# Second cross attention with halved Fourier products, and the last experts' routing done inside the last cross attention

## The reference, cut to what matters

```python
# layer 1, cross attention, on the normalised x (queries) and ctx_1024 (keys, values)
Q = (queries @ wq).reshape(Bv, Lv, H, Dh).transpose(0, 2, 3, 1)
K = (keys @ wk).reshape(Bv, Lv, H, Dh).transpose(0, 2, 3, 1)
corr = jnp.fft.irfft(jnp.fft.rfft(Q, axis=-1) * jnp.conj(jnp.fft.rfft(K, axis=-1)), n=Lv, axis=-1)
top_vals, top_idx = jax.lax.top_k(corr, k_top)          # k_top = 5
# softmax of the five, then five rolled copies of V, mixed by these weights, @ wo

# layer 3, cross attention: linear attention, 16 heads of 16
q = jax.nn.elu(q) + 1.0
k = jax.nn.elu(k) + 1.0
S = jnp.einsum('bhle,bhld->bhed', k, q)
out = jnp.einsum('bhme,bhed->bhmd', v, S)
denom = jnp.einsum('bhld,bhld->bhl', q, k) + 1e-06
return out @ Wo + bo

# layer 3, experts, on the normalised result: one of 8 experts for each token
logits = flat @ Wr
top_vals, top_idx = jax.lax.top_k(logits, TOP_K)
weights = jax.nn.softmax(top_vals, axis=-1)
top1, w_top1 = top_idx[:, 0], weights[:, 0]
h = gelu(flat @ W1[top1]); y_sel = h @ W2[top1]
out = (w_top1[:, None] * y_sel)
```

## Time and profile before

| | us |
|---|---|
| median of 3 runs | 3126.3 (3125.74 to 3130.65) |
| the profiled execution, its own time | 3151.78 |
| its span | 3149.9 |
| second cross attention, first load to the next stage | 1255.4 to 1512.9 |
| last cross attention | 2573.9 to 2763.1 |
| last experts, routing part up to the first expert product | 2763.96 to 2855.9 |
| last experts, tiles | 2855.9 to 3149.9 |

### The profile page before, as it was taken

How to read it: one execution, slowest core, us unless ns; L and a number is a source line. 1 busy time by engine, 2 the same in 40 slices (tenths; PEclk the granted TensorE clock), 3 DMA queues, 4 the chain that set the end, 5 groups by cost and what they waited for, 6 DMA issues and landing times. The chain is left out here.

```text
span 3149.9 us, 58131 instructions
## 1 busy us (share of the span) xinstructions
PE 2890.9 (92%) x20825; PEld 2309.4 (73%) x20826; DVE 1708.3 (54%) x4515; ACT 1203.7 (38%) x2278; POOL 508.5 (16%) x820
## 2 busy tenths in 40 slices
PE   7979999999997999899789789999799989977998
PEld 6866666666665888788678656666588877777998
DVE  4546777777775011577666477777322237752111
ACT  1325555555553121454334435445333223322221
POOL 1111121111110000000455401110000011041111
PEclk9989999999998999999789889999899999958999
DMA  3049900000000443100214410000111100035553
GB/s 119 0 172 393 367 2 0 0 0 0 0 0 1 171 148 119 30 17 17 85 63 145 128 40 27 20 20 1 63 54 53 54 19 1 0 145 182 178 176 122
DMA packets 126689, 246.54 MB, mean 78 GB/s; under 512 B 17132, under 2 KB 76908, under 8 KB 120176
## 3 DMA queue, kind: packets, MB, share of 16 engines
q1 hardware_dynamic: 116688, 219.72, 20.2%
q0 software_dynamic: 9888, 25.38, 2.2%
HBM read 149.14 MB, written 97.75 MB: 78 GB/s over the span
## 5 line engine op out<-in xcount | busy, mean ns | idle before, releaser
L507 DVE TENSOR_REDUCE m0hnm<-banks 128x4 f32<-128x1024 f32 x256 | 312.9, 1222 | 173.8 <-PE banks L435 173.7
L534 ACT ACTIVATE m0hpT<-banks 128x1024 f32<-128x1024 f32 x256 | 263.1, 1028 | 356.1 <-PE banks L448 356.1
L435 PE MATMUL banks<-m0hk,m0hq 32*128 32x256 f32 x2048 | 293.3, 404 | 12.1 <-DVE m0hnm L507 11.7
L448 PE MATMUL banks<-m0hq,m0hk 32*128 32x256 f32 x2048 | 292.3, 402 | 1.1 <-ACT m0hpT L534 1.1
L532 ACT ACTIVATE a2hpT<-banks,a2hlow 128x512 f32<-128x512 f32 x256 | 162.2, 684 | 191.1 <-PE banks L448 191.1
L435 PEld LDWEIGHTS banks<-m0hk,m0hq 32*128 32x128 f32 x2048 | 176.5, 186 | 64.5 <-DVE m0hnm L507 33.4
L507 DVE TENSOR_REDUCE a2hnm<-banks 128x4 f32<-128x1024 f32 x128 | 156.6, 1223 | 87.5 <-PE banks L435 87.5
L448 PEld LDWEIGHTS banks<-m0hq,m0hk 32*128 32x128 f32 x2048 | 178.2, 185 | 2.1 <-issue 1.7
L435 PE MATMUL banks<-a2hk,a2hq 32*128 32x256 f32 x1024 | 147.8, 406 | 24.7 <-DVE a2hnm L507 24.6
L3083 PEld LDWEIGHTS banks<-E3xT,E3w 128*128 128x128 f32 x1248 | 147.8, 195 | 2.0
L3083 PE MATMUL banks<-E3xT,E3w 128*128 128x128 f32 x1248 | 147.9, 278 | 0.0
(11 more groups left out here) (479 smaller groups left out, 6430.8 us busy)
## 6 DMA issues: line engine op xcount, KB each, us to landing
E3w<-in_L_ffn_W_dram SPq DMA_DIRECT2D x47, 1024.0 KB, 4.9
slots<-M0pad SPq DMA_DIRECT2D x8, 4290.0 KB, 34.4
slots_x<-M0pad SPq DMA_DIRECT2D x8, 4290.0 KB, 36.4
E0w<-in_L_ffn_fw_dram SPq DMA_DIRECT2D x64, 512.0 KB
E2w<-in_L_ffn_w_dram SPq DMA_DIRECT2D x16, 1024.0 KB
E1xin<-slots SPq DMA_DIRECT2D x71, 130.0 KB
A2routed<-routed SPq DMA_DIRECT2D x16, 512.0 KB
E3xin<-slots_x SPq DMA_DIRECT2D x39, 130.0 KB
```

The source lines that it names most:

```text
L435: ins = pe.matmul(self.scores[:, j, tc], self.q[strip(half, j), u, e, c, chunk(tc)], self.k[strip(half, j), u, e, c], start=True, stop=True)
L448: ins = pe.matmul(self.turned[:, j, kc], self.k[strip(half, j), u2, e2, c2, chunk(kc)], self.q[strip(half, j), u2, e2, c2], start=True, st ...
L507: v.tensor_reduce(self.nm[:, e, :, at:at + 33:32].rearrange("p c g -> p g c"), self.scores, AX.X, ALU.max, negate=True).then_inc(self.nm_r ...
L534: ins = a.activation(dst, self.turned, ACT.Exp)
```

## The change

**In the second cross attention** the Fourier products are split. GpSimd forms the sum and the difference of the two token halves of `xn` (into `xs`) and of the context (into `cs`). The even frequencies need only the sum and the odd ones only the difference, so each of the two products takes 128 rows in place of 256 (`halved`). The correlation goes to two PSUM banks and is copied in two halves. Statistics and normalisation of batch b+2 stand earlier in VectorE's turn. At the start each engine waits only for the loads that it needs.

**In the last layer** attention and routing are one function, `layer3`. Slot b of the attention also takes batch b-1 or b-2 through statistics, normalisation (now on ScalarE), transposes, router products, and at fixed slots through `route`, `ranks` and `place` for the groups of batches 0 to 3, 4 to 7 and 8 to 11; the rows of batches 0 to 9 are scattered in slots 7, 8, 11, 12 and 15. Batches 12 to 15 are routed in two groups of two behind a barrier, where the rows of batches 10 to 15 are scattered. All slots are written out, with no loop. GpSimd computes the reciprocal deviation before it waits for the value product. The output bias is added to `x` on GpSimd (`bias`), not on VectorE. Half of the second expert weights are loaded during the attention, into memory that the earlier layers have left.

```diff
 # layer1_attention
+            def halves(dst, src):
+                g.tensor_tensor(dst[:, 0], src[:, 0], src[:, 1], ALU.add)
+                return g.tensor_tensor(dst[:, 1], src[:, 0], src[:, 1], ALU.subtract)
+            def fold_x(b):
+                g.wait_ge(xn_rdy, b + 1)
+                if not (isinstance(b, int) and b == 0):
+                    g.wait_ge(fx_mm, b)
+                halves(xs, xn).then_inc(xs_rdy, 1)
+            def fold_c(b):
+                g.wait_ge(c_in, 16 * b + 16)
...
+                halves(cs, ctx_in).then_inc(cs_rdy, 1)
...
             def body(b, one, two):
                 if two:
                     norm(b + 2)
+                    fold_x(b + 2)
+                    fold_c(b + 2)
...
-            v.wait_ge(w_in, 16 * loads)
-            ch.start(0)
-            stats(0)
...
+                if two:
+                    stats(b + 2)
                 v.wait_ge(ex_rdy, b + 1)
...
                 ins.then_inc(blk_rdy, 1)
                 if two:
-                    stats(b + 2)
+                    apply(b + 2)
                 v.wait_ge(blkT_mm, b + 1)
...
                 if one:
                     first(b + 1)
-                if two:
-                    apply(b + 2)
...
+            def halved(j, src):
+                for m in range(C):
+                    for e in range(2):
+                        last = pe.matmul(bank(j)[:, m].rearrange("p (r e j) -> p r e j", r=2, e=2)[:, :, e], src[:, e, chunk(m)],
+                                         dft_f[:, e].rearrange("p (r j) -> p r j", r=2), start=True, stop=True)
+                return last
...
-                product(pe, lambda m: bank(0)[:, m], lambda k, m: xn[:, k, chunk(m)],
-                        lambda k: dft_f[:, k]).then_inc(fx_mm, 1)
+                halved(0, xs).then_inc(fx_mm, 1)
+                pe.wait_ge(cs_rdy, b + 1)
+                halved(1, cs).then_inc(fc_mm, 1)
 # layer3: constants
+    GROUPS = ((0, 4), (4, 8), (8, 12), (12, 14), (14, 16))
+    routed_at = {hi + 1: g for g, (lo, hi) in enumerate(GROUPS) if hi + 2 < B}
+    placed_at = {slot + 1: g for slot, g in routed_at.items()}
+    rows_at = {7: (0, 1), 8: (2, 3), 11: (4, 5), 12: (6, 7), 15: (8, 9)}
 # layer3, attention, GpSimd
+                def bias(b):
+                    g.wait_ge(fr.xn_rdy, b + 1)
+                    g.tensor_tensor(env.x[:, b], env.x[:, b], tg_bo[:].unsqueeze(1).broadcast_to([P, C, D]), ALU.add).then_inc(bias_rdy, 1)
+                for b in range(-1, B):
+                    if b + 1 < B:
+                        bias(b + 1)
+                    if b + 3 < B:
+                        fr.rstd_of(g, b + 3, (b + 3) % 2)
+                    if b >= 1:
+                        root(g, b - 1)
+                    for r in rows_at.get(b, ()):
+                        scatter(g, r)
+                    if b + 3 < B:
+                        g.wait_ge(v_mm, b + 2)
+                        fr.context(g, b + 3, (b + 3) % 2)
 # VectorE, in slot b
-                for c in range(C):
-                    last = v.tensor_tensor(y[:, u, c], T3[u][:, c], bo[:], ALU.add)
...
+                    if b >= 1:
+                        v.wait_ge(y_used, b + 2)
+                        stats(v, b - 1)
...
+                    if b in routed_at:
+                        route(v, ch, routed_at[b])
+                    if b in placed_at:
+                        place(v, ch, placed_at[b], ranked(b))
 # ScalarE, in slot b
+                    if b >= 2:
+                        rows_turned(a, b - 2, T0[nu])
...
+                    if b >= 2:
+                        take_logits(a, b - 2, T0[nu])
...
+                    if b >= 1:
+                        normalise(a, b - 1)
+                    for r in rows_at.get(b, ()):
+                        rows_of(a, r)
 # TensorE, in slot b
+                    if b >= 2:
+                        turn(pe, b - 2, T0[nu])
...
+                        logits(pe, b - 2, T0[nu])
...
+                    if b in placed_at:
+                        pe.wait_ge(lg_rdy, b - 1)
+                        ranks(pe, placed_at[b], ranked(b))
 # layer3, behind the barrier, TensorE
+                turn(pe, 14, bank(0))
+                logits(pe, 14, bank(0))
+                ranks(pe, 3, ranked(3))
+                turn(pe, 15, bank(1))
+                logits(pe, 15, bank(1))
+                ranks(pe, 4, ranked(4))
```

More of the change, by code:

```diff
@@ L1419, in take @@
                     a.wait_ge(o_mm, b)
[L1420 to L1424, removed]
+                copy(vw_mm, b + 1, vw[:], 5, vw_rdy)
+                for c in range(C):
+                    a.wait_ge(co_mm, 2 * b + c + 1)
+                    a.activation(corr[:, c, 0:S], co_bank(c), ACT.Copy).then_inc(co_rdy, 1)
             take(0)
@@ L1464, in correlate @@
                 pe.wait_ge(sp0_rdy, b + 1)
-                product(pe, lambda m: bank(4)[:, m], lambda k, m: sp_[:, k, chunk(m)],
-                        lambda k: dft_g[:, k]).then_inc(co_mm, 1)
-            pe.wait_ge(w_in, 16 * loads)
+                for m in range(C):
+                    for k in range(C):
+                        last = pe.matmul(co_bank(m), sp_[:, k, chunk(m)], dft_g[:, k], start=(k == 0), stop=(k == C - 1))
+                    last.then_inc(co_mm, 1)
             front(0)
@@ L2719, in layer3_experts @@
         side, token = sb("side", [P, N, 4]), sb("token", [P, N])
[L2720 removed]
+        lg = sb("lg", [P, N, E])
+        hot, eq, pos = (sb(n, [P, GN, E]) for n in ("hot", "eq", "pos"))
         m1, m2, wt, posf = (sb(n, [P, GN]) for n in ("m1", "m2", "wt", "posf"))
[L2722 to L2725 removed]
@@ new lines, in normalise, with rows_turned @@
+        def normalise(a, b):
+            a.wait_ge(rstd_rdy, b + 1)
+            if b >= 2:
+                a.wait_ge(xl_mm, b - 1)
+            for c in range(C):
+                last = a.activation(xf[:, b % 2, c], env.x[:, b, c], ACT.Identity, scale=rstd[:, b % 2, c:c + 1],
+                                    bias=shift[:, b % 2, c:c + 1])
+            last.then_inc(xf_rdy, 1)
+        def rows_turned(a, b, turned):
+            a.wait_ge(xl_mm, b + 1)
+            if b >= 2:
+                a.wait_ge(lg_mm, b - 1)
+            a.activation(xl[:, b % 2], turned, ACT.Copy).then_inc(xl_rdy, 1)
@@ new lines, in turn, with logits @@
+        def turn(pe, b, turned):
+            pe.wait_ge(xf_rdy, b + 1)
+            if b >= 2:
+                pe.wait_ge(xl_rdy, b - 1)
+                pe.wait_ge(lg_rdy, b - 1)
+            transpose4(pe, turned, xf[:, b % 2], env.ident[:]).then_inc(xl_mm, 1)
+        def logits(pe, b, turned):
+            pe.wait_ge(xl_rdy, b + 1)
+            for tc in range(C):
+                for k in range(C):
+                    last = pe.matmul(turned[:, 0, tc * E:tc * E + E], xl[:, b % 2, k, chunk(tc)], wr[:, k],
+                                     start=(k == 0), stop=(k == C - 1))
+            last.then_inc(lg_mm, 1)
```

1099 lines of the change are left out of this document (555 added, 544 removed).

## The result

The changed kernel takes 3078.55 us (median of 4 runs, 3077.34 to 3081.97) against 3126.02 (4 runs, 3122.35 to 3130.65): the ratio is 0.9851, 95% interval 0.9835 to 0.9867, so 47.5 us less. The forecast was 3070, 56 less.

The account below looks back on a forecast made before the run. It took TensorE's work to bound the second cross attention, and a 92 us chain without expert products the routing. Start -9, turns -9, last attention +20, routing -57.6 sum to -56: 3126.3 becomes 3070, range 3048 to 3103.

Parts of the forecast that it names:

- Start, -9: Second cross attention's start: statistics no longer wait for loads, so the stage starts 9 us earlier, between -6 and -10.
- Turn, -0.6 each, -9: Second cross attention: shorter Fourier products, less GpSimd's delay of VectorE, make a turn 13.8 us; -9 over 15 turns.
- the pair's 0.25: Second cross attention's turn: each of GpSimd's four sums delays VectorE 0.25 us, as a profiled pair beside a copy; +1.0.
- The upper bound: Second cross attention's turn: VectorE stands still through all four sums, +2.9 less slack 0.3, turn 15.7, +20 us.
- that rival: Second cross attention: shared port held whole, turn 15.7, 3090 in all; or turn 16.2 and 3100; chance 0.14.
- 13.1 without contention: Second cross attention: GpSimd's sums cost VectorE nothing, turn 13.1, stage -29, 3059 in all; chance 0.25.
- Slot, +0.75: Last cross attention: added transposes and router products partly fill the wait for `sm`; +0.75 us a slot, 14 slots, +10.
- Ranks, route, last scatters, +4 +1 +4 and bias +1: Last cross attention: ranks +4 us, `route` in three slots +1, slot 15's four scatters +4, GpSimd's bias +1.
- The ring: Last cross attention: slots become as long as a ring of waits across engines; total above 3120 us; chance 0.04.
- Tail, 34.6: Routing behind the barrier: first expert product after 34.6 us against 92.2, -57.6; SyncE and first rows' landing 14.4.
- the three named values: Second cross attention: turn of 13.1, 13.8 or 15.7 us in the profile after would settle the port question.
- the signs of being wrong: Waits on `E3xf` or `E3xl` over 1 us, TensorE or VectorE waiting for GpSimd's bias, last attention's clock below 1.00.

Follow-up runs that it names:

- the late start: Against the changed kernel, VectorE waits for all loads of the second cross attention before its first statistics, as before the change: 3080.89 us, ratio 0.986.
- the late scatters: Against the changed kernel, the four scatters of batches 8 and 9 stand behind the barrier in place of slot 15: 3069.67 us, ratio 0.9823.

## Why the prediction was right, and where it missed

The time fell in the range, 1.5 us inside its upper end, and the direction and the size of the last layer were right. Within the last layer the sums agree partly by luck, as the steps show:

- **Start, -9**: right. 8.6 by the late start, near the 7.13 us that VectorE had waited. The first product waited for GpSimd's sums of `xn`, though, and not for the landing of `dft_f` as forecast: the table had landed 2.1 us behind its issue at 1254.77, the product began at 1259.21.
- **Turn, -0.6 each, -9**: mis-sized; measured +0.06, 0 in all. The step that failed is "I take the pair's 0.25 for each of four sums". The mechanism was right, the price was not: by the products' own rows 0.26 (0.95 for 0.69), 0.52, 0.52 and 0.41, together 1.7. Of this the slack of 0.3 comes off, and 13.0 becomes 14.4 (measured 14.45). The 0.25 of the earlier trace rows came from another kind of meeting: a VectorE pair of TENSOR_SCALAR with one tile and two small scalars, beside a copy. The upper bound (VectorE stands still through all four sums, 15.7) was too high as well: a sum takes 0.73 us and held VectorE up by 0.52 at most. Nor do the times of that rival follow from its own terms: +11 in the stage, with +20 and -57.6, gives 3100 and not 3090, and a turn of 16.2 gives 3107 and not 3100. The two free ends of the sum were exact: 13.1 without contention (13.0 measured), blk's wait 0.4 (0.41).
- The Trainium skill ("SBUF — State Buffer", "Who interferes with whom") says that a VectorE instruction with at most one SBUF input, outside the modes that use two ports, does not contend with GpSimd, and one with two does with an instruction that reads SBUF. The run with the query spectrum in PSUM agrees, product by product: 0.41 with one SBUF input, 0.94 with two. The other half of the rule that the prediction cites, the port held for the whole instruction, does not price the turn: by it the turn would be 15.7, measured are 14.45.
- **Slot, +0.75**: measured +0.5 on the plain slots (11.42 against 10.85 to 11.05). **Ranks, route, last scatters, +4 +1 +4 and bias +1**: measured, slot 6 took 1.5 over a plain one, the last scatters 6.8 (by the late scatters), the bias 3.2 (by the bias on VectorE). That +20 was forecast and +20.6 measured is luck: too much for the slot, too little for scatters and bias.
- **The ring as the losing side**: it did not decide, but it was seen. Around 2670 us GpSimd issues the last of four scatters, adds the bias (1.27 us), and only then comes to the deviations and the shift. ScalarE waits 2.85 us for the shift, and TensorE, in slot 10, 1.44 for `E3xf`. A copy of one column that takes 0.18 elsewhere takes 0.89 on the way:

```profile
...
2674.59 0.89 POOL L2618 COPY E3side<-E3rstd 128x1 f32<-128x1 f32 x1
...
2676.62 1.09 ACT L2690 ACTIVATE E3xf<-x_all,E3shift,E3rstd 128x256 f32<-128x256 f32 x2 [2.85 <-POOL E3shift L2619]
...
2677.77 0.66 PE L77 MATMUL banks<-ident,E3xf 128*128 128x128 f32 x4 [1.44 <-ACT E3xf L2690]
```

- **Tail, 34.6**: the length was right and its largest piece wrong. By the forecast the scatters end at 22 us and do not limit. They ended at 23.2 (2776.87 - 2753.66), but the last one landed only at 29.4: the forecast had no term for this landing, 6.1 us behind the issue's end. The weights were issued at 20.8 and the first rows landed at 33.6, forecast 33.4, but of that stretch, taken for 14.4 us of SyncE's own work and the rows' landing, 6.9 were SyncE waiting for the scatter (from 2776.10 to 2783.05). So the sum came out by luck, with a wrong piece in it. What the tail would have taken without this wait, no run shows.

Of what the profile after was to show, the wait for `blk` (0.41), the slots' waits for `sm` and the length of the tail came out; the turn was 14.45 and none of the three named values, three long waits on `rstd` were still there (1.80, 3.00 and 1.71 us), and the largest piece of the tail was the scatter. Two of the signs of being wrong appeared, each in a small size: the waits on `E3xf` reached 1.44 (once, over the 1 us named), and GpSimd's bias cost the attention 3.2 us. The granted clock stayed at 1.00 from 2600 to 2740.

## What to carry to other kernels

Moving element-wise work from TensorE to GpSimd is not free when VectorE has two-input instructions in SBUF at that moment: price each meeting at the part of the GpSimd instruction that holds (here 0.5 of 0.73 us), and first move one operand to PSUM or the GpSimd work behind the products. GpSimd's last transfers ahead of a barrier delayed all engines (6.8 us here); behind it they lay in a gap and cost nothing. Once an engine's sum is cut, look again at what closes the loop: TensorE's work fell by 1.7 us a turn and the turn kept its length, because VectorE's five products took 1.7 longer.

## What the runs showed of the hardware that was not expected

GpSimd's sums and VectorE's products took strict turns: product by product 0.94 for 0.42, sum by sum 1.18 and 0.90 for 0.73, with neither engine held for the whole of the other's instruction. In the turn shown above their ends alternate: product 1414.36, sum 1414.96, product 1415.23, sum 1415.81, product 1416.10, sum 1416.68, product 1416.97. A sum and a product together take 0.87 us, less than their own 0.73 and 0.42 one behind the other. A GpSimd sum over 8 columns took 0.65 in place of 0.20 beside such a product. And a plain GpSimd copy of one column took 0.89 in place of 0.18 in the last attention, beside a VectorE instruction of 1.22 us with two SBUF inputs.
